# Attention front end: query and key projection in three blocks of 128 columns instead of four of 96, with thirty stack transfers

## The chip, the cores and the metric

The kernel runs on one core of one Trainium2 chip. The metric is the device time of one execution in microseconds (us), from the first to the last work of the program. One core has five engines that run their own instruction streams and wait for each other on semaphores: PE (TensorE, matmul), DVE (VectorE), ACT (ScalarE), POOL (GpSimd) and SP (SyncE, here only a queue that issues transfers).

## The reference, cut to what matters

```python
h = tok(x)                        # 5 shifted copies, 16x16 patches, layer norm, W: (64,196,192)
h = concat(h, txt)                # 324 tokens of 192 for each of 64 images
xn = norm_scale * layernorm(h) + norm_bias
q, k, v = split(xn @ W_attn + b_attn, 3)          # 12 heads of 16
q, k = rope(q), rope(k)           # pairs: o0 = x0*c - x1*s, o1 = x0*s + x1*c
att = softmax([sink, causal(q @ k.T / 4)])[..., 1:]
h = h + (att @ v @ W_proj + b_proj) * rezero
h = h + soft_moe(h)               # 64 experts, each 192 -> 768 -> 192
```

## The kernel before, in words

The kernel has two parts. The first runs over the 64 images, one at a time, and leaves residuals, combine weights and each expert's input. The second runs the 64 experts in pairs and adds their mixed outputs to the residuals. The change touches only the first.

Each engine has a function `step(b, i)` that is called for b = -3 to 64, and the order inside a step is written out by hand. In step b the engines do the attention of image b (`att`), the stacking of keys and queries of image b+1 (`mid`), the embedding, layer norm, projection and rotation of image b+2 (`front`), and the expert dispatch of image b-1 (`moe`). All four run in steps 1 to 61; attention and front together run in the 62 steps from 0 to 61.

A step on PE has three stages. First the scores of 12 heads (`scores`, L463), whose row maxima DVE takes (L983), with pieces of embedding (L420) between. Then the transposed scores (`scores_t`, L480 to L486), of which ACT takes the exponential (L705), and products with the values (L502). Then the end of the step: the last value products, four projections of queries and keys (`project`, L661), transposes of the attention output (L680), transposes of the normalized output (L523, tile `ynorm`, the same memory as `xhat`), and the output projection (L695). Lines 705 and 1099 are helpers: ACT's every activation stands at L705.

A projection is `project(side, e)`: side is query or key, e is the first or second element of a rotary pair. Each gives 96 rows (8 pairs times 12 heads) of 324 tokens in a PSUM bank of its own. It is two fp32 matmuls (K of 97 with the bias row, and of 96), and the profile shows each fp32 matmul as two records, so four projections are 16 records.

DVE multiplies both banks of a side by cosines and sines (L1078), POOL combines them into `rot` (L1167, L1168), and `rot` is then written as a sum of three bf16 parts: ACT casts (`split`, L705), POOL subtracts (L1122, L1147). SP copies the parts into the matrices `qst` and `kst`, where part, pair and element are stacked along the partitions (`stack`, L343): 6 slots times 2 elements times 2 sides are 24 transfers of an image, 12 of them for part 0, 8 for part 1 and 4 for part 2. The text rows of image b+2 are loaded (L384) between part 0 and part 1 on the same queue, ahead of it stand the image load (L329 to L332) and the copy `h_held` (L373), and behind all of it the combine weights (L398). The next step begins on SP with the residuals (L403, L404), which wait for DVE's sum `h1` (L1085, L1087).

Before the first step, `prepare` builds the window weights from five layouts of W: ACT scales the first layout by gamma (nine calls at L705), DVE adds the other four (L932), PE takes column sums (L559), and DVE subtracts the mean (L940). Only then PE embeds the first image (L420). ACT also issues the constant loads (L747) there, among them the tables of cosines and sines.

## Time and profile before

| what | value |
|---|---|
| median of 3 runs | 3040.28 us (3039.4 to 3050.72) |
| the profiled execution, its own time | 3038.94 us |
| its span | 3037.2 us |
| busy share of the span: PE, DVE, ACT, POOL | 91%, 56%, 53%, 35% |
| PE weight loads | 65% |
| q1, the transfer queue of SP: share of 16 DMA engines | 35.6% |

The profile is one execution. "Busy" is the time in which an engine had an instruction in flight. PE's records overlap, so a group's duration is longer than its share of the path: there the distance between the starts of neighbouring groups counts. The steps over the images fill the span from about 58 us to 2600 us, and the experts fill the rest.

### The profile page before, as it was taken

The page shows a single profiled execution, that of the slowest core. Times are in us where ns is not written, and L with a number is a line of the kernel's source. Part 1 is how long each engine was busy: PE and PEld are TensorE (multiplying, and loading weights), DVE is VectorE, ACT ScalarE, POOL GpSimd, SP SyncE. Part 2 cuts the span into 40 slices and gives each one's busy share as a digit, 9 for nine tenths or more (in the row PEclk, how much of TensorE's full clock was granted, in tenths as well). Part 3 has the DMA queues.
Part 4 walks back from the last instruction along what each step waited for, and adds up shares of the span by engine and source line. Part 5 has one row for each costly group of instructions (what it writes and reads, how often), then busy time and mean ns, then how long its engine had stood idle before and what let it go on. Part 6 is the DMA issues. An engine that isn't in the chain of part 4 may idle for free. (4 is left out here: it accounts for less than half of the span.)

```text
span 3037.2 us, 71306 instructions
## 1 busy us (share of the span) xinstructions
PE 2758.8 (91%) x24694; PEld 1986.3 (65%) x24694; DVE 1705.4 (56%) x7747; ACT 1606.9 (53%) x3254; POOL 1063.6 (35%) x1879
## 2 busy tenths in 40 slices
PE   5899999999999999999999999999999997688856
PEld 4577777777777777777777777777777765344423
DVE  5366666666666666666666666666666664111133
ACT  1466666666666666666666666666666653100000
POOL 3344444444444444444444444444444441000000
PEclk8899999999999999999999999999999997788877
DMA  3333333333333333333333333333333321899989
GB/s 95 81 95 95 95 95 95 95 95 95 91 96 94 93 95 94 94 93 94 94 92 95 93 93 94 94 94 93 94 91 90 93 76 31 227 274 279 275 218 303
DMA packets 367349, 354.75 MB, mean 117 GB/s; under 512 B 31660, under 2 KB 338541, under 8 KB 366990
## 3 DMA queue, kind: packets, MB, share of 16 engines
q1 hardware_dynamic: 329478, 292.45, 35.6%
q10 hardware_dynamic: 37512, 57.74, 6.3%
q8 instruction: 198, 3.24, 0.5%
q14 instruction: 161, 1.32, 0.1%
HBM read 193.84 MB, written 40.30 MB: 77 GB/s over the span
## 5 line engine op out<-in xcount | busy, mean ns | idle before, releaser
L983 DVE CUSTOM_DVE_ANT_0 ps<-ps,late 128x325 f32<-128x325 f32 (+2 forms) x2304 | 748.4, 395 | 7.6 <-PE ps L463 4.0
L705 ACT ACTIVATE prob<-ps 128x590 f32<-128x590 f32 x768 | 501.6, 661 | 186.1 <-PE ps L486 171.7
L420 PE MATMUL ps<-window_w,xp 108*98 108x193 f32 x2304 | 500.9, 336 | 3.3 <-DVE window_w L940 3.3
L463 PE MATMUL ps<-kst,qst 99*128 99x325 bf16 (+2 forms) x2304 | 330.4, 253 | 38.0 <-DVE negmax L983 31.5
L1167 POOL TENSOR_TENSOR rot<-by 96x324 f32<-96x324 f32 x128 | 111.6, 872 | 686.7 <-DVE by L1078 686.7
L420 PEld LDWEIGHTS ps<-window_w,xp 108*98 108x98 f32 x2304 | 338.2, 166 | 6.8 <-issue 4.2
L661 PE MATMUL ps<-xt,wqk 97*96 97x324 f32 (+1 forms) x1024 | 320.2, 445 | 1.7 <-ACT xt L705 1.7
L463 PEld LDWEIGHTS ps<-kst,qst 99*128 99x128 bf16 (+1 forms) x2304 | 199.4, 106 | 183.4 <-DVE negmax L983 136.5
L983 DVE DVE_READ_ACCUMULATOR2_ANT negmax<- 128x1 f32 (+1 forms) x2304 | 315.9, 137 | 0.0
L502 PE MATMUL ps<-prob,vaug 128*32 128x324 f32 (+2 forms) x4608 | 286.0, 340 | 0.0
L1065 DVE RECIPROCAL rden<-ps 98x12 f32<-98x12 f32 (+1 forms) x192 | 43.3, 226 | 385.7 <-PE ps L680 385.7
L480 PE MATMUL ps<-qst,kst 102*128 102x295 bf16 x768 | 229.2, 298 | 27.0 <-ACT prob L705 17.3
L705 ACT ACTIVATE xp<-xw 108x1764 f32<-108x1764 f32 x64 | 219.8, 3434 | 0.0
L661 PEld LDWEIGHTS ps<-xt,wqk 97*96 97x96 f32 (+1 forms) x1024 | 157.1, 165 | 83.2 <-issue 4.6
L483 PE MATMUL ps<-qst,kst 102*128 102x197 bf16 x768 | 189.9, 247 | 0.0
L480 PEld LDWEIGHTS ps<-qst,kst 102*128 102x128 bf16 x768 | 77.9, 101 | 162.7 <-issue 53.9
L1147 POOL TENSOR_TENSOR part<-by,part 96x648 bf16<-96x648 f32 x128 | 178.1, 1411 | 14.8 <-issue 8.1
L1122 POOL TENSOR_TENSOR by<-rot,part 96x648 f32<-96x648 f32 x128 | 178.4, 1413 | 0.0
L1286 PE MATMUL ps<-w,y_all 97*64 97x384 f32 (+1 forms) x512 | 118.7, 619 | 63.1 <-DMA w<-in_L_ffn_fc_bias_dram 63.1
L481 PE MATMUL ps<-ident_b,causal 128*128 128x127 bf16 x768 | 171.5, 223 | 0.0
L484 PE MATMUL ps<-ident_b,causal 128*128 128x128 bf16 x768 | 170.6, 222 | 0.0
L1354 ACT ACTIVATE hidden<-ps 128x768 f32<-128x768 f32 x32 | 26.0, 811 | 256.7 <-PE ps L1286 256.7
(195 smaller groups left out, 5632.7 us busy)
## 6 DMA issues: line engine op xcount, KB each, us to landing
xw<-in_x_dram SPq DMA_DIRECT2D x384, 189.0 KB
qst<-part SPq DMA_DIRECT2D x768, 60.8 KB
kst<-part SPq DMA_DIRECT2D x768, 60.8 KB
w<-in_L_ffn_fc_weight_dram SPq DMA_DIRECT2D x64, 576.0 KB
w<-in_L_ffn_fc_weight_dram ACTq DMA_DIRECT2D x64, 576.0 KB, 10.9
h_held<-h_new SPq DMA_DIRECT2D x64, 288.0 KB, 3.7
residual_image<-h SPq DMA_DIRECT2D x64, 147.0 KB
h_i<-residual_image SPq DMA_DIRECT2D x16, 588.0 KB
```

The costliest lines, as they stand in the source:

```text
L420: mm = pe.matmul(ps[0:TILE, BK7, half * (D + 1):(half + 1) * (D + 1)], xp[:, q, TILE * half:TILE * (half + 1)], window_w[:, q, :], start=( ...
L463: mm = pe.matmul(ps[0:nq, bk, col:col + keys], qst[i][0:MAX_ROW, h, q0:q0 + nq], kst[i][0:MAX_ROW, h, 0:keys], start=True, stop=True)
L480: pe.matmul(ps[:, bank, 0:EXPC], k0, q[:, 0:EXPC], start=True, stop=False)
L481: pe.matmul(ps[:, bank, 0:127], causal[:], ident_b[:, 1:128], start=False, stop=True)
L483: pe.matmul(ps[:, bank + 1, c1:c2], k1, q[:, KTILES[1][2]:T], start=True, stop=False)
L484: pe.matmul(ps[:, bank + 1, c1:c1 + 128], causal[:], ident_b[:], start=False, stop=True)
L502: mm = pe.matmul(ps[STRIP * s:STRIP * (s + 1), BK6, q0:T], vaug[i][0:nk, k, h, :], prob[0:nk, h % 8, col:col + T - q0], start=(k == 0), st ...
L661: mm = pe.matmul(ps[0:HALF, SC + 2 * side + e, 0:T], wqk[0:k, c, 2 * side + e, :], xt[0:k, c, 1:KEYS], start=(c == 0), stop=(c == 1))
L705: return nc.scalar.activation(out_, in_, f, **kw)
L983: last = dve.tensor_tensor_reduce(out=ps[0:nq, bk, col:col + keys], in0=ps[0:nq, bk, col:col + keys], in1=late[0:nq, gone:gone + keys], sc ...
L1122: pool.tensor_tensor(rest[:, side], rot[:, side], part[0][:, side], ALU.subtract).then_inc(rest_ready.sem, 1)
L1147: pool.tensor_tensor(part[2][:, side], rest[:, side], part[1][:, side], ALU.subtract).then_inc(p3_ready.sem, 1)
```

## The change: what it does

For each element e there are 96 query and 96 key columns (12 heads of 8 pairs). The new layout has three blocks of 128 columns: block 0 is the e=0 half of all 12 query heads and of key heads 0 to 3 (96 + 32), block 1 the e=1 half of the same, block 2 both halves of key heads 4 to 11 (64 + 64). The diff has these parts:

1. `project(g)` runs for three blocks instead of four. Block 0 stands ahead of the transposes of L680, block 1 behind them, block 2 behind the transposes of `ynorm`; before, two stood ahead of L680, one behind it, one behind `ynorm`.
2. The transposes of `ynorm` go tile by tile, each waiting for its own tile, instead of all six waiting for the last.
3. DVE's rotary products are two calls of 128 x 648 on blocks 0 and 1, and for block 2 one of 128 x 324 and two of 64 x 324 whose output lies in the other half of the partitions. POOL has three combining calls instead of four. ACT's casts and POOL's subtractions go in two waves, of 648 and of 324 columns with 128 partitions, instead of two of 648 with 96.
4. `stack` issues for each key slot three transfers (32, 32 and 128 rows) instead of two of 96: 30 an image, 15 for part 0, 10 for part 1, 5 for part 2.
5. In `prepare`, DVE scales the first layout instead of ACT, the tables take six more loads on ACT's queue (fifteen constant loads instead of nine), DVE negates half a sine table once, and `window_done` counts the nine window positions, so that PE's first embedding waits for one position at a time.

```diff
-SQ, SE = 2, 2
+SE = 2
+PACKS = 3
+LOW, HIGH = 4, 8
+MID = HIGH * PAIR
-            wqk = sb("wqk", [HALF + 1, 2, SQ * SE, HALF], F32, layers)
+            wqk = sb("wqk", [HALF + 1, 2, PACKS, 128], F32, layers)
...
-            cos_t = sb("cos_t", [HALF, T], F32, layers)
+            sin_t = sb("sin_t", [128, 2, T], F32, layers)
...
-                by = tmp("by", [128, 2, SQ, SE, T])
-                by_cos, by_sin = by[0:HALF, 0], by[0:HALF, 1]
-                rot = tmp("rot", [HALF, SQ, SE, T])
+                by = tmp("by", [128, 2, PACKS, T])
+                by_cos, by_sin = by[:, 0], by[:, 1]
+                rot = tmp("rot", [128, PACKS, T])
-                part = [tmp(f"part{i}", [HALF, SQ, SE, T], BF16) for i in range(PARTS)]
+                part = [tmp(f"part{i}", [128, PACKS, T], BF16) for i in range(PARTS)]
+                waves = (slice(0, 2), slice(2, 3))
...
-                wa = rot[:].rearrange("p s e t -> p (s e t)")[:, 0:6 * D].rearrange("p (c n) -> p c n", c=2)
+                wa = tmp("wa", [HALF, 2, 3 * D])[:]
...
-                stack_in = Signal("stack_in", 16 * 24)
+                stack_in = Signal("stack_in", 16 * 30)
...
+                def packs(e):
+
+                    low, high = D, D + LOW * HD
+                    return ((slice(0, D), NH, e, slice(0, HALF), 0.25), (slice(low, high), LOW, e, slice(HALF, 128), 1.0),
+                            (slice(high, 2 * D), HIGH, 2, slice(MID * e, MID * (e + 1)), 1.0))
...
-                    def stack(b, i, p, side):
-
-                        st, which = ((qst[i], Q_PART), (kst[i], K_PART))[side]
+                    def stack(b, i, p):
+
                         for slot in range(SLOTS):
-                            if which[slot] == p:
-                                for e in range(SE):
-                                    rows = slice(SE * slot + e, SINK_ROW, SE * SLOTS)
-                                    dst = st[rows] if side == 0 else st[rows, :, 1:KEYS]
-                                    sp.dma_start(dst, part[p][:, side, e, :]).then_inc(stack_in.sem, 16)
+                            for e in range(SE):
+                                rows = slice(SLOTS * PAIR * e + slot, SLOTS * PAIR * (e + 1), SLOTS)
+                                if Q_PART[slot] == p:
+                                    sp.dma_start(qst[i][rows], part[p][0:HALF, e]).then_inc(stack_in.sem, 16)
+                                if K_PART[slot] == p:
+                                    sp.dma_start(kst[i][rows, 0:LOW, 1:KEYS], part[p][HALF:128, e]).then_inc(stack_in.sem, 16)
+                            if K_PART[slot] == p:
+                                sp.dma_start(kst[i][slot:SINK_ROW:SLOTS, LOW:NH, 1:KEYS], part[p][:, 2]).then_inc(stack_in.sem, 16)
...
-                            stack(b + 1, 1 - i, 0, 0)
-                            stack(b + 1, 1 - i, 0, 1)
+                            stack(b + 1, 1 - i, 0)
-                            stack(b + 1, 1 - i, 1, 0)
-                        if has(b + 1):
-                            stack(b + 1, 1 - i, 1, 1)
+                            stack(b + 1, 1 - i, 1)
                             p3_ready.wait(sp, b + 1)
-                            stack(b + 1, 1 - i, 2, 0)
-                            stack(b + 1, 1 - i, 2, 1)
+                            stack(b + 1, 1 - i, 2)
...
+                        if b == 0 and half == 0:
+                            pe.wait_ge(window_done, q + 1)
                         mm = pe.matmul(ps[0:TILE, BK7, half * (D + 1):(half + 1) * (D + 1)],
...
-                        pe.wait_ge(window_done, 1)
...
-                        def project(side, e):
-                            if side == 0 and e == 0:
+                        def project(g):
+                            if g == 0:
                                 xt_ready.wait(pe, b + 2)
                                 if b == -2:
                                     pe.wait_ge(qkv_scaled, 1)
                                     pe.wait_ge(placed, 16 * 4)
-                            if e == 0:
-                                exp_ready.wait(pe, b, NH - 1 + side)
+                            if g != 1:
+                                exp_ready.wait(pe, b, NH - 1 + g // 2)
                             for c in range(2):
                                 k = HALF + 1 - c
-                                mm = pe.matmul(ps[0:HALF, SC + 2 * side + e, 0:T], wqk[0:k, c, 2 * side + e, :],
-                                               xt[0:k, c, 1:KEYS], start=(c == 0), stop=(c == 1))
-                            if e == 1:
+                                mm = pe.matmul(ps[:, SC + g, 0:T], wqk[0:k, c, g, :], xt[0:k, c, 1:KEYS],
+                                               start=(c == 0), stop=(c == 1))
+                            if g > 0:
                                 mm.then_inc(qk_mm.sem, 1)
...
-                            project(0, 0)
-                            project(0, 1)
+                            project(0)
...
-                            project(1, 0)
+                            project(1)
                         if att:
...
-                            yn_ready.wait(pe, b)
-                            turn((BK6, BK4), ynorm).then_inc(yt_mm.sem, 1)
+                            for t, (t0, nt) in enumerate(TTILES):
+                                yn_ready.wait(pe, b, t + 1)
+                                for c in range(2):
+                                    mm = pe.transpose(ps[0:HALF, (BK6, BK4)[c], t0:t0 + nt],
+                                                      ynorm[0:nt, t, HALF * c:HALF * (c + 1)], ident[0:nt, 0:nt])
+                            mm.then_inc(yt_mm.sem, 1)
                         if front:
-                            project(1, 1)
+                            project(2)
...
-                        for side in range(2):
-                            need.wait(act, b, side + 1)
-                            if side == 0:
+                        for w, wave in enumerate(waves):
+                            need.wait(act, b, w + 1)
+                            if w == 0:
                                 stack_in.wait(act, b - 1)
-                            fn(dst[:, side], src[:, side], ACT.Copy).then_inc(done.sem, 1)
+                            fn(dst[:, wave], src[:, wave], ACT.Copy).then_inc(done.sem, 1)
...
-                                (cos_t[:], cos_c), (sin_t[:], sin_c)):
+                                (cos_t[0:HALF, 0], cos_c), (sin_t[0:HALF, 0], sin_c)):
                             act.dma_start(dst, src).then_inc(const_in, 16)
-                        act.wait_ge(first_read, 1)
-                        act.wait_ge(gains_in, 16 * TAP_PIECES)
-                        for q in range(WIN2):
-                            last = fn(spread[0][:, q], spread[0][:, q], ACT.Copy, scale=tap(gains, 0, q))
-                        last.then_inc(first_scaled, 1)
+                        for table, src in ((cos_t, cos_c), (sin_t, sin_c)):
+                            by_heads = src.rearrange("(i h) t -> i h t", h=NH)
+                            act.dma_start(table[HALF:128, 0], by_heads[:, 0:LOW]).then_inc(const_in, 16)
+                            for e in range(SE):
+                                act.dma_start(table[MID * e:MID * (e + 1), 1], by_heads[:, 0:HIGH]).then_inc(const_in, 16)
...
-                        for side in range(2):
-                            for e in range(2):
+                        for e in range(SE):
+                            for cols, heads, pack, at, factor in packs(e):
                                 for c in range(2):
-                                    src = wa[:, c, D * side:D * side + D].rearrange("p (h i e) -> p i h e", h=NH, e=2)[:, :, :, e]
-                                    fn(wqk[0:HALF, c, 2 * side + e, :].rearrange("p (i h) -> p i h", h=NH), src, ACT.Copy,
-                                       scale=0.25 if side == 0 else 1.0)
+                                    src = wa[:, c, cols].rearrange("p (h i e) -> p i h e", h=heads, e=SE)[:, :, :, e]
+                                    fn(wqk[0:HALF, c, pack, at].rearrange("p (i h) -> p i h", h=heads), src, ACT.Copy, scale=factor)
                         fn(wv[0:HALF], wa[:, :, 2 * D:3 * D], ACT.Copy).then_inc(qkv_scaled, 1)
...
-                                act.wait_ge(window_done, 1)
+                                act.wait_ge(window_done, WIN2)
...
-                        dve.wait_ge(first_scaled, 1)
+                        dve.wait_ge(first_read, 1)
                         dve.wait_ge(gains_in, 16 * TAP_PIECES)
+                        for q in range(WIN2):
+                            dve.tensor_scalar(window_w[:, q, 0:D], window_w[:, q, 0:D], tap(gains, 0, q), None, ALU.mult)
                         for n in range(1, 5):
...
-                        last.then_inc(window_done, 1)
-                        dve.wait_ge(const_in, 16 * 9)
+                        dve.wait_ge(const_in, 16 * 15)
+                        dve.tensor_scalar(sin_t[MID:128, 1], sin_t[MID:128, 1], -1.0, None, ALU.mult)
+                        for e in range(SE):
+                            for cols, heads, pack, at, factor in packs(e):
+                                src = bar[:, cols].rearrange("p (h i e) -> p i h e", h=heads, e=SE)[:, :, :, e]
+                                dve.tensor_scalar(brow[:, pack, at].rearrange("p (i h) -> p i h", h=heads), src, factor, None, ALU.mult)
...
-                            for side in range(2):
-                                qk_mm.wait(dve, b + 2, side + 1)
-                                if side == 0:
-                                    rot_ready.wait(dve, b + 1)
-                                    p3_ready.wait(dve, b + 1)
-                                for table, dst in ((cos_t, by_cos), (sin_t, by_sin)):
-                                    last = dve.tensor_tensor(dst[:, side], ps[0:HALF, SC + 2 * side:SC + 2 * side + 2, 0:T],
-                                                             table[:].unsqueeze(1).broadcast_to((HALF, SE, T)), ALU.mult)
-                                last.then_inc(rope_ready.sem, 1)
+                            qk_mm.wait(dve, b + 2, 1)
+                            rot_ready.wait(dve, b + 1)
+                            p3_ready.wait(dve, b + 1)
+                            for table, dst in ((cos_t, by_cos), (sin_t, by_sin)):
+                                last = dve.tensor_tensor(dst[:, 0:2], ps[:, SC:SC + 2, 0:T],
+                                                         table[:, 0].unsqueeze(1).broadcast_to((128, SE, T)), ALU.mult)
+                            last.then_inc(rope_ready.sem, 1)
+                            qk_mm.wait(dve, b + 2, 2)
+                            dve.tensor_tensor(by_cos[:, 2], ps[:, SC + 2, 0:T], cos_t[:, 1], ALU.mult)
+                            for src, dst in ((slice(MID, 128), slice(0, MID)), (slice(0, MID), slice(MID, 128))):
+                                last = dve.tensor_tensor(by_sin[dst, 2], ps[src, SC + 2, 0:T], sin_t[src, 1], ALU.mult)
+                            last.then_inc(rope_ready.sem, 1)
...
+                            for w, wave in enumerate(waves):
+                                p1_ready.wait(pool, b + 1, w + 1)
+                                pool.tensor_tensor(rest[:, wave], rot[:, wave], part[0][:, wave], ALU.subtract
                                                    ).then_inc(rest_ready.sem, 1)
...
-                            for side in range(2):
-                                rope_ready.wait(pool, b + 2, side + 1)
-                                pool.tensor_tensor(rot[:, side, 0], by_cos[:, side, 0], by_sin[:, side, 1], ALU.subtract)
-                                pool.tensor_tensor(rot[:, side, 1], by_sin[:, side, 0], by_cos[:, side, 1], ALU.add
-                                                   ).then_inc(rot_ready.sem, 1)
+                            rope_ready.wait(pool, b + 2, 1)
+                            pool.tensor_tensor(rot[:, 0], by_cos[:, 0], by_sin[:, 1], ALU.subtract)
+                            pool.tensor_tensor(rot[:, 1], by_sin[:, 0], by_cos[:, 1], ALU.add).then_inc(rot_ready.sem, 1)
+                            rope_ready.wait(pool, b + 2, 2)
+                            pool.tensor_tensor(rot[:, 2], by_cos[:, 2], by_sin[:, 2], ALU.add).then_inc(rot_ready.sem, 1)
```

The end of a step on PE, before: `ps<-xt,wqk` is the projection, `ident,yraw` the transposes of L680, `ident,xhat` those of `ynorm`, `wp,yt` the output projection, and `kst,qst` the first scores of the next step.

```order
L502 MATMUL ps<-prob,vaug 32x69 x4
L661 MATMUL ps<-xt,wqk 96x324 x4
L680 MATMUL ps<-ident,yraw 98x128 x6
L680 MATMUL ps<-ident,yraw 128x128 x3
L661 MATMUL ps<-xt,wqk 96x324 x2
L523 MATMUL ps<-ident,xhat 96x98 x2
L523 MATMUL ps<-ident,xhat 96x128
L523 MATMUL ps<-ident,xhat 96x98 x2
L523 MATMUL ps<-ident,xhat 96x128
L661 MATMUL ps<-xt,wqk 96x324 x2
L695 MATMUL ps<-wp,yt 98x192 x4
```

And the same place with the change.

```order
L512 MATMUL ps<-prob,vaug 32x69 x4
L670 MATMUL ps<-xt,wqk 128x324 x2
L688 MATMUL ps<-ident,yraw 98x128 x6
L688 MATMUL ps<-ident,yraw 128x128 x3
L670 MATMUL ps<-xt,wqk 128x324 x2
L697 MATMUL ps<-ident,xhat 96x98 x4
L697 MATMUL ps<-ident,xhat 96x128 x2
L670 MATMUL ps<-xt,wqk 128x324 x2
L707 MATMUL ps<-wp,yt 98x192 x4
```

One projection (two matmuls) is gone from ahead of L680, now L688; the rest stands in the same order.

SP's queue from the copy `h_held` to the text load, before:

```order
L373 DMA h_held<-h_new 128x576
L343 DMA qst<-part 8x12x324 x6
L343 DMA kst<-part 8x12x324 x6
L384 DMA h_new<-in_txt_dram 128x192
L343 DMA qst<-part 8x12x324 x4
```

And with the change:

```order
L385 DMA h_held<-h_new 128x576
L351 DMA qst<-part 8x12x324
L353 DMA kst<-part 8x4x324
L351 DMA qst<-part 8x12x324
L353 DMA kst<-part 8x4x324
L355 DMA kst<-part 16x8x324
L353 DMA kst<-part 8x4x324 x2
L355 DMA kst<-part 16x8x324
L353 DMA kst<-part 8x4x324 x2
L355 DMA kst<-part 16x8x324
L351 DMA qst<-part 8x12x324 x4
L395 DMA h_new<-in_txt_dram 128x192
```

The text load now stands behind 15 transfers of the stack instead of 12.

## Rows read from the trace of the kernel before

**Rows 1.** Busy time in the stretch 1000 to 2000 us: PE, PEld, DVE, ACT, POOL, clock.

```profile
1000.00:2000.00 1000.00, 965.39 (x9256) 717.66 (x9255) 639.20 (x3042) 638.29 (x1300) 421.10 (x755) 1.00 0.34 94
```

**Rows 2.** SP's queue in order of time: start us, us, engine, line, operation.

```profile
1077.49 0.34 SPq L403 DMA_DIRECT2D residual_image<-h  x1
...
1086.18 4.68 SPq L343 DMA_DIRECT2D qst<-part  x6
...
1095.28 0.38 SPq L384 DMA_DIRECT2D h_new<-in_txt_dram  x1
...
1102.88 1.39 SPq L343 DMA_DIRECT2D kst<-part  x2
...
1230.88 0.34 SPq L403 DMA_DIRECT2D residual_image<-h  x1
```

**Rows 3.** PE in order of time, the end of one step.

```profile
1027.39 0.73 PE L523 MATMUL ps<-ident,xhat 98*96 98x98 f32 x6
...
1029.18 2.42 PE L661 MATMUL ps<-xt,wqk 97*96 97x324 f32 x8
1031.45 1.15 PE L680 MATMUL ps<-ident,yraw 128*98 128x128 f32 x9
1032.43 1.26 PE L661 MATMUL ps<-xt,wqk 97*96 97x324 f32 x4
1033.84 0.77 PE L523 MATMUL ps<-ident,xhat 98*96 98x98 f32 x6
1034.44 1.25 PE L661 MATMUL ps<-xt,wqk 97*96 97x324 f32 x4
1035.54 2.12 PE L695 MATMUL ps<-wp,yt 97*98 97x192 f32 x12
```

**Rows 4.** The waits between 1000 and 2000 us: total us, times, longest.

```profile
PEld ps L463 <- DVE negmax L983: 52.6, 157, 0.4
```

**Rows 5.** DVE in order of time, same step, and its norm in the next.

```profile
1024.96 0.96 DVE L1057 TENSOR_SCALAR xhat<-h_new,mv,rstd 98x192 f32<-98x192 f32 x3 [1.00 <-POOL rstd L1099]
1031.98 0.23 DVE L1065 RECIPROCAL rden<-ps 98x12 f32<-98x12 f32 x1 [6.05 <-PE ps L680]
...
1033.70 0.82 DVE L1078 TENSOR_TENSOR by<-ps,cos_t 96x648 f32<-96x648 f32 x1
...
1035.74 0.83 DVE L1078 TENSOR_TENSOR by<-ps,cos_t 96x648 f32<-96x648 f32 x1 [0.48 <-PE ps L661]
...
1037.70 0.56 DVE L1085 TENSOR_TENSOR h<-ps,h_held 98x384 f32<-98x384 f32 x1 [0.39 <-PE ps L695]
...
1060.92 0.88 DVE L883 BATCH_NORM_STATS2 bn<-h_new 98x6 f32<-98x192 f32 x3
```

**Rows 6.** ACT in order of time, same step.

```profile
1029.65 3.44 ACT L705 ACTIVATE xp<-xw 108x1764 f32<-108x1764 f32 x1
1034.64 0.76 ACT L705 ACTIVATE yt<-ps 96x324 f32<-96x324 f32 x2 [1.55 <-PE ps L523]
```

**Rows 7.** The text load's line over the whole span.

```profile
DMA to landing us min/median/max: 1.8/2.0/3.5
```

**Rows 8.** Preparation and first steps in order of time: DVE, POOL, ACT, PE.

```profile
24.75 3.00 DVE L924 TENSOR_SCALAR lexp<-lexp,sn,scl 64x192 f32<-64x192 f32 x1
...
59.35 0.30 DVE L961 TENSOR_SCALAR wp<-wp,rz 97x192 f32<-97x192 f32 x1
...
100.06 0.88 DVE L883 BATCH_NORM_STATS2 bn<-h_new 98x6 f32<-98x192 f32 x3 [3.30 <-DMA h_new<-in_txt_dram]
...
24.30 6.73 POOL L1188 MEMSET qst<- 32x3888 bf16 x2
...
31.29 3.51 POOL L1190 MEMSET y_all<- 1x4096 f32 x1
...
35.62 3.22 ACT L705 ACTIVATE window_w<-window_w,h 108x192 f32<-108x192 f32 x9
...
57.87 5.43 PE L420 MATMUL ps<-window_w,xp 108*98 108x193 f32 x16 [3.31 <-DVE window_w L940]
```

More of the change, by code:

```diff
@@ L1144, in step @@
                             stack_in.wait(pool, b)
-                            for side in range(2):
-                                p2_ready.wait(pool, b + 1, side + 1)
-                                pool.tensor_tensor(part[2][:, side], rest[:, side], part[1][:, side], ALU.subtract
+                            for w, wave in enumerate(waves):
+                                p2_ready.wait(pool, b + 1, w + 1)
+                                pool.tensor_tensor(part[2][:, wave], rest[:, wave], part[1][:, wave], ALU.subtract
                                                    ).then_inc(p3_ready.sem, 1)
```

19 lines of the change are left out of this document (6 added, 13 removed).

## The prediction, made before the changed kernel ran

> **What bounds the kernel now.** I read the busy table of a stretch in the middle first: PE is busy for 965 of 1000 us at full clock, and no other engine for more than 640 [rows 1]. Next the period: SP's residual transfer starts at 1077.49 and, four steps later, at 1230.88, so a step takes 38.35 us [rows 2]. Then I followed the end of one step on PE [rows 3] and on DVE [rows 5], since the change works there. The reader should see a chain that goes back and forth: the transposes of L680 start at 1031.45, DVE normalizes three tiles from 1031.98 to 1033.70, PE transposes them from 1033.84, ACT copies them (`yt`, 1034.64 to 1035.40, [rows 6]), PE projects the output from 1035.54, and DVE adds the residual at 1037.70, with 0.39 idle before it that PE ended. From there DVE goes on with its norm and the next scores, and PE's score stage waits for DVE's maxima (157 waits, 52.6 us in 26 steps, [rows 4]). So the step is set by PE's end of step plus DVE's run behind it. Whatever makes L695 end earlier moves both, and the score stage with them.
>
> **The projections.** Eight records of two projections stand between 1029.18 and 1031.45, 2.27 us, so one projection of four records costs 1.13 [rows 3]. The change keeps the 324 moving columns of a record and takes 16 records down to 12: one projection less ahead of L680. Off the path: 1.13 us a step. The trace has no fp32 record of 324 columns on 128 weight columns in this place. The price lies between the 1.13 of today and 4/3 of it, if a record cost by its output columns; I take 1.13, as the spacing is that of the columns streamed.
>
> **The wait for `ynorm`.** The third projection starts at 1032.43 and ends 1.13 later, at 1033.56, but L523 starts at 1033.84: 0.28 us of waiting for DVE. With L680 at 1030.32, DVE starts its tiles at 1030.85 and ends at 1032.57. PE ends block 1 at 1032.43, turns tiles 0 and 1 (two thirds of the 0.60 between 1033.84 and 1034.44) until 1032.83, and finds tile 2 there. The wait goes. What is late next is ACT: its copy of the image (`xp`) ends at 1033.09 [rows 6], and the turned tiles are ready to copy at about 1033.23, so 0.14 is left. `yt` then takes 0.76, until 1033.99, and block 2 covers that until 1034.13. So L695 starts at 1034.13 instead of 1035.54, 1.41 earlier. With spares of 0.1 that jitter will eat now and then, I take **1.33 a step**.
>
> **DVE's rotary products.** On blocks 0 and 1 they are two calls as now (0.82 each), started at 1032.63 when block 1 is done, and end by 1034.27. Block 2 is there at 1034.33 (0.20 behind PE, as in 1035.54 to 1035.74, [rows 3, 5]). Its three calls of 324 columns are not in the trace: between 0.23 (the smallest call there) and 0.83 (648 columns) each. I take 0.45, half the columns and some overhead: 1.35, until 1035.68. The residual sum is due 2.16 behind L695's start, at 1036.29, so it costs nothing. At 0.83 each it would come 0.54 late. POOL loses one call of four and a quarter of the split work, and ACT as much; neither is on the path, so this counts zero.
>
> **The six transfers.** On SP, 24 stack transfers with the text load among them run from 1086.18 to 1104.27. Without the load's 0.43 that is 0.736 each [rows 2]. The new ones have 32 or 128 rows instead of 96. Bounds are zero and, as the largest one that these rows allow, the 0.78 of the first six (4.68); I take 0.736. Text load: it starts 17.8 after L403 and lands 2.0 later [rows 7], so at 19.8. DVE's norm needs it at 1060.92, 22.3 after the sum of 1037.70 was done (1038.6). Of the 2.5 spare, three more transfers take 2.2. Behind that, `xhat` is ready at 1025.92 and PE turns it at 1027.39, another 1.5. Cost zero. End of the stack: 26.8 behind L403 today, 31.2 with six more (4.4), 33.2 with the landing. The next scores start one microsecond before the next sum, 36.0 behind this one in a step of 37.0. Spare 2.8, cost zero.
>
> **The preparation.** ACT ends its nine calls on the first layout at 38.84 and DVE waits for them, free since 27.75 [rows 8]. If DVE scales at 0.30 a call from 27.75, it is done at 30.45: 8.4 us gained. But the row of 24.75 speaks against that: this DVE call took 3.00, where its like at 59.35 took 0.30. It ended at 27.75, when the first of POOL's two memsets (24.30, 6.73 for both) did. The nine new calls would meet the second memset, until 31.03, and after it the one from 31.29 to 34.80. If POOL and DVE take turns, one call runs at 31.03, one behind POOL's small memset, and seven from 35.1: done at 37.2, a gain of 1.7. The Trainium skill (SBUF — State Buffer, Who interferes with whom) says just this of a tensor_scalar within SBUF: it can take the port pair that VectorE shares with GpSimd, and whoever issues first keeps it for the whole instruction. By that rule the term is 1.7, without it 8.4; the row agrees with the rule. I take 1.7. ACT's own work there (six more loads, four more small casts) ends about where it did. Waiting for one window position instead of nine lets PE start when the first of DVE's nine calls is done: eight ninths of the 3.31 that it idled [rows 8] are 2.9, of which I take 2.7. Against that, step -1 is set by the text load behind part 0 (DVE idle 3.30 before 100.06): three more transfers, 2.2 lost. The projection missing in step -1 gives 1.1. Together **3.3 us gained**, with 0 and 11 as its ends.
>
> **The sum.** 62 steps have attention and front: 62 x 1.33 = 82.5, and 3.3 make 85.8. From the profiled execution's own 3038.94 this gives **2953 us**. The median of the runs is 1.3 above that execution, well inside the range. A measurement of this kernel can tell about 0.5% (15 us) from no change.
>
> **Rivals.**
> *The rotary products of block 2 become the end of the step.* For it: they stand behind the last projection and the residual sum stands behind them on DVE. Against: 0.6 spare at my price. At 0.83 each the sum comes 0.54 late, the gain is 0.8 a step: 62 x 0.8 and 3 give 2986.
> *The stack becomes the bound, and the kernel slower.* Place: SP's queue between `h_held` and the last key transfer. It starts with this step's residual sum, and the next scores wait for its last landing. Price: per transfer. Spare is 2.8 us, so it costs from 0.83 a transfer, and from 0.87 all of the 1.33 is gone ((22.1 + 2.8 + 1.3) / 30). For it: the first six after the image load already take 0.78. Against: the last two of part 2 take 0.70 (1.39 for both) without a queue ahead of them, and the new shapes move the same bytes. If the 18 key transfers took 1.0 each, the stack would be 4.7 longer, 1.9 late; a step would be 0.6 longer than now: 3039 + 62 x 0.6 - 3 = 3073. The text load would be late only behind that.
> *The blocks are no cheaper.* If a record costs by its 128 output columns, 12 of them cost what 16 of 96 did, and only the wait of about 0.2 goes: 3039 - 12 - 3 = 3024. Nothing in the rows is for it.
> *The preparation gains all it can.* Should DVE's nine calls slip in without POOL, and each step gain the full 1.41 and a little more, the time is near 2935.
>
> **How the numbers follow.** My forecast has 0.74. Its own range is 62 x 1.13 with no gain ahead (2969) to 62 x 1.45 with 11 (2938). The late products have 0.10, the stack as bound 0.07, blocks no cheaper 0.05, and a result below the range 0.04. The range goes from 2936 to 2990, which takes in the forecast and the first rival and leaves out less than 2 in 10. Faster by over 0.5%: 0.74 + 0.10 + 0.04 = 0.88. Within 0.5%: 0.05. Slower: 0.07.
>
> **What the profile after would show.** Right: 12 projection records a step with the same 0.28 between starts; no idle time of PE before the transposes of `ynorm`; L707 some 5 us behind block 0's start instead of 6.4 (1029.18 to 1035.54); a step of 37.0 between two residual transfers; 30 stack transfers of about 0.74, and no wait of PE's scores for a landing in `kst` or `qst`; DVE calls on the first layout some of which last 3 us beside POOL's memsets. Wrong: a transfer above 0.83, DVE waiting at its norm for the text in every step, the residual sum with no idle time before it (products late), or `yt` waiting for ACT's `xp`.

## The result and the profile after

The changed kernel takes 2941.01 us, the median of 4 runs (2939.78 to 2942.66), against 3039.92 for the kernel before on the same chip: ratio 0.9667, interval 0.9645 to 0.9689. The forecast was 2953, 12 us too high. The profiled execution took 2939.78 (span 2938.0), 99.2 us less of span than before.

The stretch 1000 to 2000 us of the kernel after: the stretch and its length, then busy us of PE, PEld, DVE, ACT and POOL, clock, DMA share, GB/s.

```profile
1000.00:2000.00 1000.00, 969.34 (x9515) 738.46 (x9515) 663.13 (x3191) 650.72 (x1350) 392.27 (x757) 1.00 0.36 98
```

PE is as full as it was [rows 1]: 969 against 965 us. So the kernel is bound by the same engine, and it is faster because a step holds less PE work. How long the step is shows in SP's queue, in order of time:

```profile
993.06 0.34 SPq L411 DMA_DIRECT2D residual_image<-h  x1
...
1001.72 0.73 SPq L351 DMA_DIRECT2D qst<-part  x1
...
1012.69 0.38 SPq L395 DMA_DIRECT2D h_new<-in_txt_dram  x1
...
1023.41 0.60 SPq L355 DMA_DIRECT2D kst<-part  x1
...
1030.01 0.35 SPq L411 DMA_DIRECT2D residual_image<-h  x1
```

From one residual transfer to the next are 36.95 us, where [rows 2] gave 38.35. The stack's first transfer starts 8.7 after the residual transfer, its last one ends 31.0 after it, so the queue has room until the next. Over 61 steps the mean fell from 38.47 to 37.01, by 1.46.

The end of a step on PE, in order of time, answers to [rows 3]:

```profile
1022.05 1.36 PE L670 MATMUL ps<-xt,wqk 97*128 97x324 f32 x4
1023.25 1.15 PE L688 MATMUL ps<-ident,yraw 128*98 128x128 f32 x9
1024.23 1.26 PE L670 MATMUL ps<-xt,wqk 97*128 97x324 f32 x4
1025.33 0.74 PE L697 MATMUL ps<-ident,xhat 98*96 98x98 f32 x6
1025.90 1.26 PE L670 MATMUL ps<-xt,wqk 97*128 97x324 f32 x4
1027.00 2.12 PE L707 MATMUL ps<-wp,yt 97*98 97x192 f32 x12
```

A block of 128 columns lasts 1.26, as a projection of 96 did. L697 starts 1.10 after block 1 began, so PE no longer waits there. L707 starts 4.95 after block 0; before it was 6.36.

DVE and ACT at the same place:

```profile
1023.77 0.23 DVE L1078 RECIPROCAL rden<-ps 98x12 f32<-98x12 f32 x1 [4.98 <-PE ps L688]
...
1025.52 0.83 DVE L1089 TENSOR_TENSOR by<-ps,cos_t 128x648 f32<-128x648 f32 x1
...
1027.20 0.49 DVE L1093 TENSOR_TENSOR by<-ps,cos_t 128x324 f32<-128x324 f32 x1
1027.70 1.00 DVE L1095 TENSOR_TENSOR by<-ps,sin_t 64x324 f32<-64x324 f32 x2
...
1029.16 0.56 DVE L1101 TENSOR_TENSOR h<-ps,h_held 98x384 f32<-98x384 f32 x1 [0.45 <-PE ps L707]
```

```profile
1022.52 3.44 ACT L717 ACTIVATE xp<-xw 108x1764 f32<-108x1764 f32 x1
1026.10 0.77 ACT L717 ACTIVATE yt<-ps 96x324 f32<-96x324 f32 x2
```

The three products of block 2 end at 1028.70, and DVE then idles 0.45 until PE gives it the sum. ACT ends `xp` at 1025.96 and starts `yt` at 1026.10. L707 starts 0.13 after `yt` is copied.

Two waits of the stretch 1000 to 2000 us, total, times, longest. The first is new; the second stood at 52.6 and 157 [rows 4]:

```profile
DVE bn L894 <- DMA h_new<-in_txt_dram: 5.4, 7, 1.1
...
PEld ps L473 <- DVE negmax L996: 54.8, 163, 0.4
```

The preparation, DVE, POOL, ACT, PE in order of time, as in [rows 8]:

```profile
24.75 3.00 DVE L935 TENSOR_SCALAR lexp<-lexp,sn,scl 64x192 f32<-64x192 f32 x1
27.68 8.83 DVE L940 TENSOR_SCALAR window_w<-window_w,h 108x192 f32<-108x192 f32 x9
36.59 6.19 DVE L945 SCALAR_TENSOR_TENSOR window_w<-prob,h,window_w 108x192 f32<-108x192 f32 x18
...
93.94 0.88 DVE L894 BATCH_NORM_STATS2 bn<-h_new 98x6 f32<-98x192 f32 x3 [6.19 <-DMA h_new<-in_txt_dram]
...
24.30 6.73 POOL L1204 MEMSET qst<- 32x3888 bf16 x2
...
31.40 3.62 POOL L1206 MEMSET y_all<- 1x4096 f32 x1
...
45.25 3.42 ACT L717 ACTIVATE xp<-xw 108x1764 f32<-108x1764 f32 x1
...
51.89 2.84 PE L430 MATMUL ps<-window_w,xp 108*98 108x193 f32 x16 [0.60 <-DVE window_w L953]
...
106.15 0.42 PE L473 MATMUL ps<-kst,qst 99*128 99x325 bf16 x3 [0.60 <-DVE by L1089]
```

The first scores stand at 106.15; before they stood at 113.31. **Where the 99.2 us are:**

| part of the span | us less |
|---|---|
| until the first scores | 7.2 |
| step 0 | 4.7 |
| 61 steps at 1.458 | 88.9 |
| the last two steps | 1.2 |
| the experts' part, behind the last residual transfer | -2.8 |

Step 0 is more than a step's share. Three windows of the kernel before, 5 us each, columns as above, the clock third from the end:

```profile
120.00:125.00 5.00, 4.13 (x41) 2.04 (x39) 5.00 (x33) 2.02 (x4) 1.81 (x5) 1.00 0.35 91
125.00:130.00 5.00, 4.41 (x22) 3.60 (x23) 2.88 (x18) 0.00 (x0) 2.71 (x6) 0.57 0.37 98
130.00:135.00 5.00, 5.00 (x42) 3.91 (x42) 0.32 (x1) 2.77 (x5) 0.00 (x0) 0.75 0.32 87
```

The profile after has 1.00 in all three. A second profile of the unchanged kernel after (it ran again beside the last experiments) shows that this is no effect of the change:

```profile
120.00:125.00 5.00, 5.00 (x27) 3.97 (x26) 0.42 (x4) 1.32 (x2) 0.87 (x4) 0.50 0.36 95
```

0.50 is the lower level, 1.2 GHz, in a stretch in which PE was busy throughout. Between 116 and 118 us, ahead of the fall, PE had been busy for 1.50 of the 2 us in both executions, so what it did there does not tell them apart. That execution had its first scores at 106.10, and its first residual transfer 3.0 later than the other one. So about 3 of step 0's 4.7 came by the execution. The last line of the table is of that kind too: from the last residual transfer to the end of the span, the 14 profiled executions of this study took 454.0 to 472.2 us, the kernel after itself 460.2 and 465.4. The experts' PE work waits there for weights (70.6 us at L1302 after, 63.1 at its L1286 before), and nothing of it was changed.

### The profile page after: what moved, and what is told of

It reads as the page before. It is cut to its first block and busy times, and to the rows that moved or that the text cites. A ratio compares the mean times of both kernels' runs of the same rounds, so it can differ in the third digit from the quotient of the medians.

```text
span 2938.0 us, 71190 instructions
## 1 busy us (share of the span) xinstructions
PE 2667.4 (91%) x24438; PEld 1961.6 (67%) x24438; DVE 1710.9 (58%) x7823; ACT 1574.7 (54%) x3249; POOL 954.8 (32%) x1815
## 5 line engine op out<-in xcount | busy, mean ns | idle before, releaser
L670 PE MATMUL ps<-xt,wqk 97*128 97x324 f32 (+1 forms) x768 | 251.3, 450 | 1.7 <-ACT xt L717 1.7
L1182 POOL TENSOR_TENSOR rot<-by 128x324 f32<-128x324 f32 x64 | 56.3, 879 | 589.0 <-DVE by L1089 589.0
L1302 PE MATMUL ps<-w,y_all 97*64 97x384 f32 (+1 forms) x512 | 119.2, 621 | 70.6 <-DMA w<-in_L_ffn_fc_bias_dram 70.6
L670 PEld LDWEIGHTS ps<-xt,wqk 97*128 97x128 f32 (+1 forms) x768 | 133.2, 193 | 43.1 <-issue 2.9
L1396 DVE COPY act_t<-ps 128x768 f32<-128x768 f32 x32 | 30.7, 958 | 211.2 <-PE ps L1312 211.2
L495 PE MATMUL ps<-qst,kst 102*128 102x69 bf16 x768 | 151.7, 197 | 0.0
```

The lines of the kernel that those rows point to most:

```text
L495: pe.matmul(ps[:, bank + 1, c2:EXPC], k2, q[:, KTILES[2][2]:T], start=True, stop=False)
L670: mm = pe.matmul(ps[:, SC + g, 0:T], wqk[0:k, c, g, :], xt[0:k, c, 1:KEYS], start=(c == 0), stop=(c == 1))
L1302: mm = pe.matmul(ps[B * j:B * (j + 1), bank + h, 0:FH], y_all[0:kk, c, 2 * n + j, :], w1[2 * p + j][0:kk, c, FH * h:FH * (h + 1)], start=( ...
```

## Experiments

Theory A is the prediction's sum, with the step's 1.41 split in two: 1.13 for the projection, the rest for the wait that went. Each experiment's mean step is over 61 steps, and its ratio is to the kernel before on the same chip.

### The two parts of the step, one at a time

**Block 0 projected twice, in the kernel after.**

```diff
                         if front:
                             project(0)
+                            project(0)
```

> Changed kernel, but PE projects block 0 twice in every step, so that it issues 16 projection records again, while the blocks, the 30 transfers and the work of DVE, ACT and POOL stay as changed. Theory A (the gain is PE time at the end of the step): four records cost 1.13 us, a step goes from 36.95 to about 38.1, in all 62 x 1.13 = 70 us more, about 3011. Rival B (the gain comes from the relief of POOL, ACT and DVE or from the transfers): stays near 2941.

Measured: 3013.83 us, ratio 0.9922 (0.9891 to 0.9952). The step is 38.11, 1.10 longer. PE at the end of the step:

```profile
1013.85 2.45 PE L670 MATMUL ps<-xt,wqk 97*128 97x324 f32 x8
1016.14 1.15 PE L689 MATMUL ps<-ident,yraw 128*98 128x128 f32 x9
```

Two blocks ahead of L689 take 2.29 from start to start, where two projections of 96 columns took 2.27 [rows 3]. One block had 1.20 (1022.05 to 1023.25), so the additional four records of 128 weight columns cost 1.09. Work put back ahead of the transposes comes back in full.

**Half of the queries' contraction left out, in the kernel before.** Four records fewer ahead of L680, in the old layout:

```diff
-                            for c in range(2):
+                            for c in range(1 + side):
...
-                                               start=(c == 0), stop=(c == 1))
+                                               start=(c == 0), stop=(c == side))
```

> Kernel before, but the two query projections leave out the second half of their contraction (4 records a step), with everything else as before: 96-row blocks, 24 transfers, the transposes of the normalized output in one go. It computes wrong queries. Theory A: 1.13 a step less, 38.35 to 37.2, about 2970; the wait of 0.28 before the transposes of the normalized output stays. Rival B: about 3040.

Measured: 2968.84 us, ratio 0.9766 (0.9731 to 0.9802); the step is 37.37, 1.09 shorter. The same price from the other side, with neither new layout nor new transfers.

**The kernel before with the `ynorm` transposes tile by tile.**

```diff
-                            yn_ready.wait(pe, b)
-                            turn((BK6, BK4), ynorm).then_inc(yt_mm.sem, 1)
+                            for t, (t0, nt) in enumerate(TTILES):
+                                yn_ready.wait(pe, b, t + 1)
+                                for c in range(2):
+                                    mm = pe.transpose(ps[0:HALF, (BK6, BK4)[c], t0:t0 + nt],
+                                                      ynorm[0:nt, t, HALF * c:HALF * (c + 1)], ident[0:nt, 0:nt])
+                            mm.then_inc(yt_mm.sem, 1)
```

> Kernel before, with nothing but the transposes of the normalized output tile by tile. Theory A: PE's wait of 0.28 is filled by the first two tiles, 0.28 a step, 17 us, about 3023. Rival C (the wait is hidden, since ACT's copy or the last projection sets when the output projection starts): about 3040.

Measured: 3015.64 us, ratio 0.9925 (0.99 to 0.995); the step is 38.13, 0.34 shorter.

**The kernel after with all six transposes behind one wait** (the same edit undone).

> Changed kernel, with the six transposes of the normalized output waiting for the last tile again. Theory A: DVE's last tile is ready 0.26 behind the end of PE's block 1, so PE waits about 0.3 a step, 19 us, about 2960. Rival C (hidden): about 2941.

Measured: 2966.19 us, ratio 0.9756 (0.9728 to 0.9783); the step is 37.37, 0.36 longer. The wait is back, here on PE:

```profile
1034.21 0.77 PE L533 MATMUL ps<-ident,xhat 98*96 98x98 f32 x6 [0.16 <-DVE xhat L1076]
```

These four close the sum of the step: 1.09 or 1.10 for the projection and 0.34 or 0.36 for the turn make 1.43 to 1.46, and 1.458 was measured. The two parts add, and no third one is needed; a kernel with both undone at once was not run. The turn is worth more than the wait of 0.28 between block and transposes: the whole turn has 0.77 as its row, the tiles 0.74, and between the starts of the transposes and of block 2 are 0.61 and 0.57 (1034.21 to 1034.82; 1025.33 to 1025.90).

### The six transfers, and how much room SP's queue has

**The kernel before with 30 stack transfers:** two of 48 rows for one of 96, on six of the twelve key transfers.

```diff
-                                    sp.dma_start(dst, part[p][:, side, e, :]).then_inc(stack_in.sem, 16)
+                                    if side == 0 or e == 0:
+                                        sp.dma_start(dst, part[p][:, side, e, :]).then_inc(stack_in.sem, 16)
+                                    else:
+                                        for j in range(2):
+                                            first = SE * slot + e + j * SE * SLOTS * PAIR // 2
+                                            sp.dma_start(st[first:first + SE * SLOTS * PAIR // 2 - e - SE * slot:SE * SLOTS, :, 1:KEYS],
+                                                         part[p][HALF // 2 * j:HALF // 2 * (j + 1), side, e, :]
+                                                         ).then_inc(stack_in.sem, 16)
```

> Kernel before, with 30 stack transfers instead of 24 (one of the two transfers of each key slot in two halves of 48 rows), and nothing else. Theory A (SP has room): steps stay at 38.35, the text load three transfers later costs about 2 us once, in step -1; about 2 us over before. Rival D (the additional transfers cost time in every step, and the changed kernel would be faster still without them): 0.3 us or more a step, 20 us or more over before.

Measured: 3040.35 us, ratio 1.0 (0.9983 to 1.0018); the step is 38.44 against 38.47. Six transfers more cost nothing. DVE's norm waited for the text 15.0 us in all, 21 times between 200 and 2300 us, and the steps did not grow: the wait was taken up behind it.

**The kernel after with 36:** block 2's transfer of 128 rows in two of 64.

```diff
-                                sp.dma_start(kst[i][slot:SINK_ROW:SLOTS, LOW:NH, 1:KEYS], part[p][:, 2]).then_inc(stack_in.sem, 16)
+                                for e in range(SE):
+                                    rows = slice(SLOTS * PAIR * e + slot, SLOTS * PAIR * (e + 1), SLOTS)
+                                    sp.dma_start(kst[i][rows, LOW:NH, 1:KEYS], part[p][MID * e:MID * (e + 1), 2]).then_inc(stack_in.sem, 16)
```

> Changed kernel, with the 128-row transfer of each key slot in two of 64 rows, 36 transfers. Each slot then costs 2 x 0.72 instead of 0.64, 4.8 us a step more on SP. In the changed kernel the last one is issued 30.95 us behind the residual store; 4.8 more and 2.0 of landing make 37.75, and the next sum follows the scores' start by 1.0. Theory A (the end of the stack becomes the bound there, by the threshold of the prediction): steps of about 38.8, with PE's scores waiting for a landing; about 3050. Rival E (the text load is what binds first, the stack has more room): steps of 37.4 to 37.6, about 2975.

Measured: 3009.93 us, ratio 0.9892 (0.9869 to 0.9916). The step is 38.01, 1.00 longer, though the best was 37.01. That lies between what the two theories expected. Its waits, 1000 to 2000 us:

```profile
DVE bn L896 <- DMA h_new<-in_txt_dram: 56.8, 26, 3.6
...
PEld ps L475 <- DMA kst<-part: 11.6, 19, 1.6
...
PE ps L475 <- DMA kst<-part: 5.3, 9, 1.3
```

The norm waits for the text in all but one of the 61 steps (26 times in the stretch), and the scores wait for the last key transfers in some. A pair of 64 rows takes 1.35 from start to start where one of 128 took 0.64, so the queue is 4.3 us longer at its end and 2.1 at the text load.

It is the text load that binds first, as rival E had it. Taken step by step over the 61, the time above 36.95 equals the norm's wait less 1.51, to within 0.02, in 32 steps: one of 37.77 has a wait of 2.33, one of 38.01 a wait of 2.57. Over all 61 steps, what the wait has above 1.51 adds up to 42 of the 64 us by which they are longer than 36.95. The 1.5 that costs nothing is the time that the prediction found between `xhat` and its transposes. Another 14 us lie in seven steps of 40.3 to 43.7, in which the norm waited for 2.9 to 3.7. In each of them, and in no other of the 61, the granted clock fell. In the first, PE had sat idle for 0.83 and 0.68 just before:

```profile
328.00:330.00 2.00, 2.00 (x20) 0.88 (x22) 0.00 (x0) 0.77 (x2) 0.00 (x0) 0.50 0.24 65
```

The other 8 us are spread over the remaining steps, some of which have the scores waiting for keys. So the run shows what a late text load costs, and not how much room the end of the stack had by itself. At 0.9892, about two thirds of the change's gain are lost (the run below, with 30 transfers, has 0.9671).

**The order of the transfers,** in each part queries first and then keys, in the kernel after:

```diff
                                 if Q_PART[slot] == p:
                                     sp.dma_start(qst[i][rows], part[p][0:HALF, e]).then_inc(stack_in.sem, 16)
+                        for slot in range(SLOTS):
+                            for e in range(SE):
+                                rows = slice(SLOTS * PAIR * e + slot, SLOTS * PAIR * (e + 1), SLOTS)
                                 if K_PART[slot] == p:
```

> Changed kernel, with all query transfers of a part ahead of its key transfers, as before. The steps of the kernel before are 38.35 at best and 38.47 in the mean, those of the changed one 36.95 and 37.01: single steps are longer where the first transposed scores wait for the maxima's transfer. Theory F (the interleaved order with its smaller transfers lets the maxima's transfer through): the mean goes back to 0.12 over the best, 4 us. Rival G (order does not matter): no difference.

Measured: 2939.87 us, ratio 0.9671 (0.9644 to 0.9698); the step is 37.01. The order is worth nothing: with room left, it does not matter which piece lands first.

**The text load behind nine transfers of the stack instead of 15:**

```diff
-                            stack(b + 1, 1 - i, 0)
+                            stack(b + 1, 1 - i, 0, (0, 1, 2))
...
+                            stack(b + 1, 1 - i, 0, (3, 4, 5))
```

> Changed kernel, with the text load ahead of the last six of the fifteen transfers of part 0. Theory A: DVE's waits for the text (6.19 us in step -1, up to 1.1 in a quarter of the steps) shrink or go; in step -1 the scores of image 0 then wait for the end of the stack instead, so 1 to 4 us less than the changed kernel. Rival H: SP waits for the copy of the held rows to land ahead of the text load, the stack ends later, no gain or a loss.

Measured: 2935.64 us, ratio 0.9645 (0.9626 to 0.9665), not to be told from the kernel after; the step is 37.00. The norm no longer waits in any step, and nothing is gained, so the few waits seen above were off the path. In step -1, DVE's norm comes 1.5 earlier, and the scores do not:

```profile
92.44 0.88 DVE L895 BATCH_NORM_STATS2 bn<-h_new 98x6 f32<-98x192 f32 x3 [3.06 <-DMA h_new<-in_txt_dram]
...
106.03 0.43 PE L474 MATMUL ps<-kst,qst 99*128 99x325 bf16 x3 [1.83 <-DMA kst<-part]
```

They start at 106.03 (106.15 before the edit), now behind the stack: step -1 has text and stack within 2 us of each other.

### The preparation

The four below ran together. The kernel after, as it is, gave 2942.66 there (ratio 0.9692, 0.9675 to 0.9709).

> The changed kernel once more, beside the three that vary its preparation, so that they are compared on the same chip. Expected: ratio to the kernel before 0.967, as measured.

**ACT scales the first layout again,** the rest as after:

```diff
+                        for q in range(WIN2):
+                            last = fn(spread[0][:, q], spread[0][:, q], ACT.Copy, scale=tap(gains, 0, q))
+                        last.then_inc(first_scaled, 1)
...
-                            dve.tensor_scalar(window_w[:, q, 0:D], window_w[:, q, 0:D], tap(gains, 0, q), None, ALU.mult)
```

> Changed kernel, with ACT scaling the first layout again, behind its fifteen constant loads. Theory A (the preparation runs through this step): ACT's table load ends at 40.9, the nine calls at 44.1, so DVE starts on the other layouts at 44.2 instead of 36.6, and the whole program comes 7 to 8 us later than the changed kernel. Rival I (hidden, since ACT's copy of the first image ends at 48.7 anyway): 3 us or less.

Measured: 2953.6 us, ratio 0.9728 (0.9709 to 0.9747), 11 more than the kernel after beside it, where 7 to 8 were expected. Each of the two ratios is known to 5 or 6 us only, and the trace agrees with the expectation. DVE waits for ACT, which has 15 constant loads to issue first:

```profile
43.51 6.17 DVE L948 SCALAR_TENSOR_TENSOR window_w<-prob,h,window_w 108x192 f32<-108x192 f32 x18 [15.76 <-ACT window_w L717]
```

43.51 against 36.59, 6.9 later; the first scores are at 113.89, 7.8 later than in the second profile of the kernel after (106.10). The step is the same 37.01. So moving the scaling is what keeps the six new loads from costing: with ACT scaling, the changed kernel has its first scores where the kernel before had them (113.31).

**POOL's memsets ahead of its wait for `slot_sq`,** so that they run before DVE scales:

```diff
-                        pool.wait_ge(slot_sq, 1)
-                        pool.tensor_tensor(sn[:], sn[:], half_c[:], ALU.pow).then_inc(slot_norm, 1)
...
+                        pool.wait_ge(slot_sq, 1)
+                        pool.tensor_tensor(sn[:], sn[:], half_c[:], ALU.pow).then_inc(slot_norm, 1)
```

> Changed kernel, with POOL's four memsets ahead of its wait for the slots' squares, where it idled from 14.1 to 23.7, instead of behind it. Theory J (POOL's memsets hold up DVE's scaling calls): the nine calls take 2.7 instead of 8.8 us, DVE's sums end 8 us earlier, and PE's first embedding starts with the end of ACT's copy of the image, 3 us earlier than in the changed kernel; about 3 us less in all. Rival K (the calls are long for a reason of their own): still about 8.8 us for nine, no gain.

Measured: 2940.2 us, ratio 0.9693 (0.9672 to 0.9714), no change that can be told. DVE and PE in the preparation:

```profile
25.55 0.37 DVE L935 TENSOR_SCALAR lexp<-lexp,sn,scl 64x192 f32<-64x192 f32 x1
25.84 2.14 DVE L940 TENSOR_SCALAR window_w<-window_w,h 108x192 f32<-108x192 f32 x9
...
48.13 5.44 PE L430 MATMUL ps<-window_w,xp 108*98 108x193 f32 x16 [6.96 <-ACT xp L717]
```

Without a memset beside them, the nine calls took 2.14 instead of 8.83, and the call before them 0.37 instead of 3.00. Same instructions, same data: POOL's memsets held them up. DVE was done 8.5 earlier, but PE starts its embedding only 3.8 earlier, because it now waits for ACT's `xp`, which stands behind the same 15 loads. Its first 16 records then take 5.44 instead of 2.84 (granted clock 0.64 in the window 50 to 55 us, where the profile after has 1.00), so the first scores are 2.6 earlier (103.54).

**That, with the six table loads issued in step -3 instead, and the text load early as above:**

```diff
-                        for table, src in ((cos_t, cos_c), (sin_t, sin_c)):
-                            by_heads = src.rearrange("(i h) t -> i h t", h=NH)
-                            act.dma_start(table[HALF:128, 0], by_heads[:, 0:LOW]).then_inc(const_in, 16)
-                            for e in range(SE):
-                                act.dma_start(table[MID * e:MID * (e + 1), 1], by_heads[:, 0:HIGH]).then_inc(const_in, 16)
...
+                        if b == -3:
+                            for table, src in ((cos_t, cos_c), (sin_t, sin_c)):
...
```

> Changed kernel with three edits: POOL's memsets early as in the run beside it, the text load ahead of six transfers of part 0, and the six additional table loads behind ACT's first copy of the image instead of ahead of the scaling of the weights. Theory A: the copy ends at about 43.4 instead of 48.7, the first squares at about 50 instead of 56, so the steps begin 6 us earlier; 6 to 9 us less than the changed kernel. Rival L (the first steps are set by SP's queue of image loads and stack transfers, which does not move as much): 0 to 3 us less.

Measured: 2930.24 us, ratio 0.9654 (0.963 to 0.9678), the lowest median of the study, 12 below the kernel after beside it; but its five runs go from 2921.38 to 2942.79, and the intervals overlap by a hair. The trace is plainer, though it does not part the three edits: PE starts its embedding at 44.03 and the first scores at 96.33:

```profile
96.33 0.68 PE L474 MATMUL ps<-kst,qst 99*128 99x325 bf16 x3 [2.22 <-DMA kst<-part]
```

9.8 us earlier, of which the first residual transfer keeps 6.6 (against the profile after) or 9.6 (against its repetition). The step is 37.00.

## Why the prediction was right, and where it was off

- **The projections: right.** 12 records at the price of 96 columns: 1.09 to 1.10 a projection against the 1.13 taken. The rival of records that cost by their output columns is out.
- **The wait for `ynorm`: right to the hundredth.** L707 was to stand 4.95 after block 0, and does. ACT's `xp` ends 0.14 before `yt` starts, as worked out.
- **1.33 a step: too small.** 0.08 was taken off the 1.41 for jitter. Measured are 1.40 between undisturbed steps and 1.46 in the mean. The jitter was in the kernel before as well: its mean step was 0.13 above its shortest one, and after it is 0.07. Of the 23 steps before that were over 0.1 longer than the shortest, 12 have PE's score stage waiting for `mt`'s copies into `qst`; after, it is 3 of 12. Those waits, of weight loads and of matmuls, came to 44.7 and 6.6 us between 200 and 2300 us before, and 35.0 and 1.6 after. 0.13 x 62 is 8 us, most of the miss. Why these waits became fewer is not shown, and they need not be the cause: in the kernel with the queries first they were 42.8 and 4.6 at the same step.
- **The rotary products: right.** The three calls took 0.49 and twice 0.50, 1.5 in all, against 1.35 taken; the sum still had 0.45 of idle time before it. That rival had 0.6 of room and used 0.15.
- **The transfers: free, for the reason given.** From start to start 0.72 for 32 rows and 0.64 for 128, against the 0.736 taken and the 0.83 from which it would have cost. The end of the stack has 3.0 of room by the prediction's own reckoning (31.0 and 2.0 to land, against 36.0), where it had 2.8. One sentence of that rival was wrong: that the text load "would be late only behind that". With 36 transfers the text load was what made the steps longer, while the stack's end can have cost no more than 8 of the 64 us. At 30 transfers the norm did wait for the text in some steps, and the 1.5 behind it, which the prediction had also found, covered all but the longest of these waits.
- **The preparation: 7.2 until the first scores instead of 3.3.** DVE was done at 36.51 where 37.2 was worked out from POOL and DVE in turns, and the profile has nearly that pattern: two of the nine calls were long (3.47 and 3.64), one beside each long memset, and one of 0.50 ran beside the small one. Six were left behind the last memset, 0.23 from start to start, where seven at 0.30 had been reckoned. So DVE starts the next stage 2.4 earlier instead of 1.7 (38.95 to 36.59). Starting by position gave 2.71 (3.31 of idle time to 0.60), where 2.7 was taken. The text cost 1.4 instead of 2.2, the missing projection gave 1.0 instead of 1.1. The rest, some 2.5, is in no term: PE's groups in the preparation ran at the higher clock for more of their time. The column sums took 4.74 instead of 5.66, and L420's 5.43 became 2.84 [rows 8], of which 1.1 reached the next group. Where L420's group stood, the granted clock was 1.00 after (51 to 57 us) and 0.53 before (57 to 63 us). Nothing in the prediction foresaw this part of the gain.
- **The port rule.** The Trainium skill (SBUF — State Buffer, Who interferes with whom) says that a tensor_scalar within SBUF can take the port pair shared with GpSimd, and that the first to issue keeps it for its whole instruction. The trace agrees: 8.83 with the memsets beside it, 2.14 without. The 8.4 that the forecast set beside it, for the case without such waiting, is the 8.5 by which DVE was done earlier with the memsets out of the way, and it would have been wrong as a gain: ACT's `xp` was the next to be late, and 2.6 was left.

The profiled execution's 2939.78 lies 13 below the 2953. Term by term: 8 in the 61 steps, 4 until the first scores, 3 in step 0 and 1 in the last two steps, less 3 in the experts' part. Most of step 0's (3 of its 4.7 by the second profile) and the experts' part are not of the change.

## What to carry to other kernels

A small fp32 matmul here costs by the columns it streams, not by the weight columns it fills, so packing four projections of 96 columns into three of 128 takes a quarter of that work away. Price a shorter path as the distance between starts, then undo each part alone: two parts that add to the whole leave little room for another cause. A queue has a limit at every transfer that somebody waits for: reckon the room at each, and the wait that the work behind it can take up (1.5 us here). And before paying for an engine's help in a preparation, see which other engine ends next; 8.5 us saved on DVE were worth 2.6 until ACT's queue was cleared too.

## What the runs showed of the hardware

- Issue on SP's queue costs by the transfer: 0.68 for 32 rows as for 96, 0.60 for 128 rows in blocks of 8 x 324, whatever the bytes.
- A DVE call whose output lies in the other half of the partitions (64x324, PSUM in) took 0.50, the one of 128x324 in place 0.49: no price for the move.
- The granted clock in the first steps differs from one execution of the same kernel to the next (1.00 and 0.50 in the window 120 to 125 us), with PE busy for all 5 us in both, and for 1.50 of the 2 us from 116 to 118 in both. What decides it stays open.
- A queue that is too long by a little did not lengthen every step alike: with 36 transfers the best step was 37.01 and the mean 38.01. Waits for the text up to 1.5 us cost nothing, longer ones their excess, and in seven steps a wait of 2.9 to 3.7 was followed by a fall of the granted clock to 0.50 and a step of over 40 us.
